# Attention in head pairs: row-tiled scores, plain fp32 attend on column tiles, normalising moved to the output

## The reference, cut to what matters

```python
q2 = (q @ wiq.T + biq).reshape(N, H, D).transpose(1, 0, 2)     # N = 384, H = 16, D = 64
k2 = (k @ wik.T + bik).reshape(N, H, D).transpose(1, 0, 2)
v2 = (v @ wiv.T + biv).reshape(N, H, D).transpose(1, 0, 2)
scores = jnp.einsum('hnd,hmd->hnm', q2, k2) * scale + mask[None]
attn = jax.nn.softmax(scores, axis=-1)
out = jnp.einsum('hnm,hmd->hnd', attn, v2)
out = out.transpose(1, 0, 2).reshape(N, OUT_F)
return out @ wo.T + bo
```

## Time and profile before

| what | value |
|---|---|
| runs | 538.48, 543.7, 538.8 us; median 538.8 us |
| profiled execution: span from first to last instruction | 537.0 us; what lies around it is not in the profile, and the median of the runs is 1.8 us above the span |
| busy PE / DVE / ACT / POOL over the span | 93% / 74% / 53% / 35% |
| mean granted clock of PE | 0.970 |
| end of half(11) to first matmul of the output projection | about 223.5 to 294.2 us |

### The profile page before, as it was taken

How to read it: one execution, slowest core, us unless ns; L and a number is a source line. 1 busy time by engine, 2 the same in 40 slices (tenths; PEclk the granted TensorE clock), 3 DMA queues, 4 the chain that set the end, 5 groups by cost and what they waited for, 6 DMA issues and landing times.

```text
span 537.0 us, 6836 instructions
## 1 busy us (share of the span) xinstructions
PE 496.9 (93%) x2583; PEld 439.1 (82%) x2583; DVE 399.3 (74%) x654; ACT 283.2 (53%) x406; POOL 189.5 (35%) x164
## 2 busy tenths in 40 slices
PE   3899999999999999999999999758999999999984
PEld 2899999999999987788888887646887877877772
DVE  5756989954444345589886875887898898898985
ACT  3443342423424225498886215436788688688630
POOL 5100443665564102288885822150020000000462
PEclk9999999999999999999999998759999999999988
DMA  8359566442334532302006362366869889888453
GB/s 303 134 213 385 120 264 239 158 158 89 147 94 150 194 105 78 131 1 79 1 1 234 125 237 99 136 241 233 320 249 422 342 340 414 344 304 361 162 191 119
DMA packets 21073, 106.33 MB, mean 198 GB/s; under 512 B 4864, under 2 KB 5248, under 8 KB 11312
## 3 DMA queue, kind: packets, MB, share of 16 engines
q1 hardware_dynamic: 15472, 91.53, 44.9%
q0 software_dynamic: 3696, 7.96, 4.5%
q10 hardware_dynamic: 1872, 6.39, 4.0%
HBM read 98.97 MB, written 6.91 MB: 197 GB/s over the span
## 4 chain that ended last, share of the span: by engine, by line
PE 56%; DVE 26%; ACT 9%; DMA 4%; issue 3%; POOL 1%; SPq 0%; ACTq 0%; DVEq 0%
PE ps L1156 51%; DVE lo L748 15%; ACT xg L665 3%; PE ps L1220 3%; ACT hi L569 3%; DMA raw<-in_wg 2%; DVE eqt L835 1%; ACT xg_hi L669 1%; DMA xg<-z_rows,slot_tok 1%; DVE x2sg L1069 1%; DMA z_rows<-xfb 1%; DVE small L753 1%; PE ps L1264 1%; ACT x2sg L674 1%; DVE ht_lo L1028 1%
## 5 line engine op out<-in xcount | busy, mean ns | idle before, releaser
L748 DVE TENSOR_TENSOR lo<-raw,hi 128x2048 fp32r<-128x2048 f32 x70 | 161.7, 2332 | 46.8 <-ACT hi L569 46.6
L569 ACT ACTIVATE hi<-raw 128x2048 fp32r<-128x2048 f32 x70 | 131.6, 1912 | 68.8 <-PE ps L1156 57.4
L454 POOL DMA_INDIRECT mask_rows<-colf,bits x48 | 61.8, 1287 | 93.7 <-DVE bits L843 44.2
L481 POOL TENSOR_SCALAR pr<-pr,small 128x384 f32<-128x384 f32 x48 | 59.1, 1249 | 53.5 <-DVE small L857 53.5
L1156 PE MATMUL ps<-xt_hi,hi 128*128 128x384 f32 x192 | 65.4, 341 | 2.2 <-DVE xt_lo L764 2.2
L1156 PE MATMUL ps<-xt_lo,hi 128*128 128x384 f32 x192 | 65.2, 339 | 0.0
L1156 PE MATMUL ps<-xt_hi,lo 128*128 128x384 f32 x192 | 65.1, 339 | 0.0
L1156 PE MATMUL ps<-hi,xg_hi 128*128 128x512 f32 x128 | 51.6, 403 | 5.7 <-DVE lo L748 3.9
L1156 PE MATMUL ps<-hi,xg_lo 128*128 128x512 f32 x128 | 50.9, 397 | 0.0
L1156 PE MATMUL ps<-lo,xg_hi 128*128 128x512 f32 x128 | 50.8, 397 | 0.0
L1156 PE MATMUL ps<-t_hi,hi 128*128 128x384 f32 x128 | 43.1, 337 | 0.6 <-DVE t_lo L794 0.6
(11 more groups left out here) (212 smaller groups left out, 1045.9 us busy)
## 6 DMA issues: line engine op xcount, KB each, us to landing
raw<-in_wf SPq DMA_DIRECT2D x42, 1024.0 KB, 7.0
raw<-in_wg SPq DMA_DIRECT2D x28, 1024.0 KB
xfb<-in_wf SPq DMA_DIRECT2D x6, 1024.0 KB, 7.4
src_i<-in_srcb ACTq DMA_DIRECT2D x4, 768.0 KB, 4.2
dst_i<-in_dstb ACTq DMA_DIRECT2D x4, 768.0 KB, 8.7
y_rows<-y SPq DMA_DIRECT2D x6, 512.0 KB, 3.0
xin<-in_x SPq DMA_DIRECT2D x3, 512.0 KB, 4.7
xres<-in_x SPq DMA_DIRECT2D x3, 512.0 KB, 4.1
```

What stands on the lines that cost most here:

```text
L454: pool.indirect_dma_start(out=mbuf[:, :], out_offset=bass.IndirectOffsetOnAxis(ap=bits[:, 1, g:g + 1], axis=0), in_=colf[:, 5, g:g + 1], i ...
L481: pool.tensor_scalar(pr[:, h % 3, i, :], pr[:, h % 3, i, :], rinv[:, h % 3, i:i + 1], None, ALU.mult).then_inc(normalised, 1)
L569: act.activation(hi[SLOT[c]][:, :], raws[RAW[c]], ACT.Copy).then_inc(hi_done, 1)
L748: dve.tensor_tensor(lo[SLOT[c]][:, :], raws[RAW[c]], f32(hi[SLOT[c]][:, :]), ALU.subtract).then_inc(lo_done, 1)
```

## The change

The unit of the loop becomes a pair of heads p, heads 2p and 2p+1, called a = 0 and 1.

- `scores(p, i)`: for one tile of 128 query rows, the matmuls of the two heads alternate. Head 0 uses contraction rows 0 to 63 of the array, head 1 rows 64 to 127, and they write two different banks. There are two pairs of score banks. The three tiles of a pair are issued at different places of the loop.
- `turn(p)`: eighteen transposes of `pr`, which is no longer divided by the sums, in six blocks over three banks. ACT copies blocks 0, 2, 4 out, and DVE blocks 1, 3, 5, whole, as fp32 `at`: there is no hi and lo of P any more.
- `attend(p)`: six plain fp32 matmuls of 384 columns with the 64 value columns of one head as weights; head 0 writes PSUM partitions 0 to 63 and head 1 partitions 64 to 127 of one bank, `SUMMED`. v is kept whole (`val`), copied by ACT and DVE.
- The reciprocals of a pair are stored by SP to memory as rows, a store of 768 elements of 4 bytes, and read back as a broadcast over 64 partitions for each head (`inv_rows`). DVE multiplies the attended pair with them (`on`), and `t_hi` and `t_lo` are written from that for all 128 rows at once. POOL's divisions are gone.
- SP's loop over the pairs stands ahead of the residual loads. Chunk 26 of the weights is split after the attention, no longer during it, and the load of chunk 29 moves behind the residual loads.

```diff
-            for c in range(GNN_CHUNKS + 2):
+            for c in range(GNN_CHUNKS + 1):
                 load(c)
...
+            for p in range(PAIRS):
+
+                sp.wait_ge(inverse_ready, p + 1)
+                sp.dma_start(ibuf[p].rearrange("a (i q) -> q a i", q=P), rinv[:, p % 2, :, :],
+                             allow_slow_non_contiguous=True).then_inc(inverse_out, 16)
+                sp.wait_ge(inverse_out, 16 * (p + 1))
+                if p >= 2:
+                    sp.wait_ge(o_scaled, p - 1)
+                for a in range(2):
+                    sp.dma_start(inv_rows[HD * a:HD * (a + 1), p % 2, :], ibuf[p, a].partition_broadcast(HD)).then_inc(inverse_in, 16)
             sp.wait_ge(score_ready, NT * HEADS)
...
+            load(GNN_CHUNKS + 1)
...
-            for h in range(HEADS):
-                for i in range(NT):
-                    if i < 2:
-                        pool.wait_ge(inverse_ready, 2 * h + i + 1)
-                    pool.tensor_scalar(pr[:, h % 3, i, :], pr[:, h % 3, i, :], rinv[:, h % 3, i:i + 1], None,
-                                       ALU.mult).then_inc(normalised, 1)
...
+            for p in range(PAIRS + 1):
+                if p < PAIRS:
+                    for m, a, j in blocks(p)[0::2]:
+                        act.wait_ge(p_turned, m + 1)
+                        act.activation(at[:, a, j, :], TURNED[j][:, 0:N], ACT.Copy).then_inc(at_act, 1)
+                if p >= 1:
+                    act.wait_ge(o_scaled, p)
+                    act.activation(t_hi[:, p - 1, :], on[:, :], ACT.Identity, bias=gbias[:, 5, p - 1:p]).then_inc(o_hi_done, 1)
+                if p + 1 < PAIRS:
+                    exps(p + 1, 2)
+                if p + 2 < PAIRS:
+                    exps(p + 2, 0)
+                    exps(p + 2, 1)
+            split_hi(OUT_LAST - 1)
             split_hi(OUT_LAST)
...
+            maxima(1, 1)
+            for p in range(PAIRS + 1):
+                if p < PAIRS:
+                    for m, a, j in blocks(p)[1::2]:
+                        dve.wait_ge(p_turned, m + 1)
+                        dve.tensor_copy(at[:, a, j, :], TURNED[j][:, 0:N]).then_inc(at_dve, 1)
+                if p >= 1:
+                    dve.wait_ge(o_ready, p)
+                    dve.wait_ge(inverse_in, 32 * p)
+                    if p >= 2:
+                        dve.wait_ge(o_lo_done, p - 1)
+                    dve.tensor_tensor(on[:, :], SUMMED[:, 0:N], inv_rows[:, (p - 1) % 2, :], ALU.mult).then_inc(o_scaled, 1)
+                if p + 1 < PAIRS:
+                    maxima(p + 1, 2)
+                if p + 2 < PAIRS:
+                    maxima(p + 2, 0)
+                if p >= 1:
+                    dve.wait_ge(o_hi_done, p)
+                    dve.scalar_tensor_tensor(out=t_lo[:, p - 1, :], in0=on[:, :], scalar=gbias[:, 5, p - 1:p], in1=f32(t_hi[:, p - 1, :]),
                                              op0=ALU.add, op1=ALU.subtract).then_inc(o_lo_done, 1)
+                if p + 1 < PAIRS:
+                    inverse(p + 1)
+                if p + 2 < PAIRS:
+                    maxima(p + 2, 1)
+            split_lo(OUT_LAST - 1)
             split_lo(OUT_LAST)
             split_lo(GNN_CHUNKS)
...
+            def scores(p, i):
+
+                n, tok = NT * p + i, slice(i * P, (i + 1) * P)
+                if n >= 2:
+                    pe.wait_ge(score_max, 2 * (n - 1))
+                for step, (s, m) in enumerate(((0, 0), (0, 1), (1, 0))):
+                    for a in range(2):
+                        rows = slice(HD * a, HD * (a + 1))
+                        ins = pe.matmul(SCORES[n % 2][a][:, 0:N], (q_hi, q_lo)[s][rows, p, tok], (k_hi, k_lo)[m][rows, p, :],
+                                        start=step == 0, stop=step == 2)
+                        if step == 2:
+                            ins.then_inc(score_ready, 1)
+
+            def turn(p):
+                pe.wait_ge(exp_done, 6 * (p + 1))
+                for m, a, j in blocks(p):
+                    if m >= 3:
+
+                        pe.wait_ge((at_act, at_dve)[(m - 3) % 2], (m - 3) // 2 + 1)
+                    for i in range(NT):
+                        ins = pe.transpose(TURNED[j][:, i * P:(i + 1) * P], pr[:, p % 2, a, i, j * P:(j + 1) * P], ident[:, :])
+                    ins.then_inc(p_turned, 1)
+
+            def attend(p):
+
+                if p >= 1:
+                    pe.wait_ge(o_scaled, p)
                 for j in range(NT):
+                    for a in range(2):
+                        m = 6 * p + 3 * a + j
+                        pe.wait_ge((at_act, at_dve)[m % 2], m // 2 + 1)
+                        cut = slice((2 * p + a) * HD, (2 * p + a + 1) * HD)
+                        ins = pe.matmul(SUMMED[HD * a:HD * (a + 1), 0:N], val[:, j, cut], at[:, a, j, :], start=j == 0, stop=j == NT - 1)
                 ins.then_inc(o_ready, 1)
...
+            scores(0, 0)
+            half(11, (0, 1))
+            pe.wait_ge(v_act, 1)
+            pe.wait_ge(v_dve, 1)
+            scores(0, 1)
+            half(11, (2, 3))
+            scores(0, 2)
+            half(11, (4, 5))
+            scores(1, 0)
+            half(11, (6, 7))
+            scores(1, 1)
+            scores(1, 2)
+            pe.wait_ge(v_act, 4)
+            pe.wait_ge(v_dve, 2)
+            for p in range(PAIRS):
+                turn(p)
+                if p + 2 < PAIRS:
+                    scores(p + 2, 0)
+                attend(p)
+                if p + 2 < PAIRS:
+                    scores(p + 2, 1)
+                    scores(p + 2, 2)
```

More of the change, by code:

```diff
@@ L45 @@
 HD = D // HEADS
+PAIRS = HEADS // 2
 EDGES = 6144
@@ L307, in gnn_ffn, with blocks @@
         TOK_BANK = [B[2], B[4]] + [B[7]] * (NE - 2)
-        SCORES, TURNED = B[3:6], [B[1], B[2], B[0]]
+        SCORES, TURNED, SUMMED = [(B[0], B[7]), (B[1], B[2])], B[4:7], B[3]
         def banks(group):
-            if group == 11:
-                return [B[6], B[7], B[0]]
+            if group >= 10:
+                return B[1:4] if group == 10 else B[4:7]
             return B[0:4] if group % 2 == 0 else B[4:8]
+        def blocks(p):
+            return [(6 * p + 3 * a + j, a, j) for a in range(2) for j in range(NT)]
         X_HALVES = [(half, t) for half in range(2) for t in range(NT)]
@@ L589, in evac @@
                 if NAMES[m] == "v2":
-                    for t in range(NT):
-                        act.activation(v_hi[:, t, h * CW:(h + 1) * CW], banks(group)[t][:, :], ACT.Copy).then_inc(bank_hi, 1)
+                    for t in (0, 2):
+                        act.activation(val[:, t, h * CW:(h + 1) * CW], banks(group)[t][:, :], ACT.Copy).then_inc(v_act, 1)
                     return
@@ L1174, in weight, with half @@
                 return hi[SLOT[c]][:, w], lo[SLOT[c]][:, w]
-            def half(i, parts=(0, 1)):
+            def half(i, steps=range(KT)):
                 m, h = HALVES[i]
@@ L1180, in half @@
                     pe.wait_ge(group_evacuated, group - 1)
-                for part in parts:
+                for part in range(2):
+                    if part * CK not in steps and (part + 1) * CK - 1 not in steps:
+                        continue
                     c = 2 * i + part
@@ L1191, in half @@
                         k = CK * part + kk
+                        if k not in steps:
+                            continue
                         if NAMES[m] == "v2":
                             for t in range(NT):
[L1194 to L1195 removed]
                                 tok = slice(t * P, (t + 1) * P)
@@ L1214, in turn @@
-            def turn(h):
-                pe.wait_ge(normalised, NT * (h + 1))
-                for j in range(NT):
-                    if h > 0:
-                        pe.wait_ge(at_lo_done, 3 * (h - 1) + j + 1)
-                    for i in range(NT):
-                        ins = pe.transpose(TURNED[j][:, i * P:(i + 1) * P], pr[:, h % 3, i, j * P:(j + 1) * P], ident[:, :])
-                    ins.then_inc(p_turned, 1)
-            def attend(h):
-                if h >= 2:
-                    pe.wait_ge(o_lo_done, h - 1)
-                pair = slice((h // 2) * P, (h // 2 + 1) * P)
-                for j in range(NT):
-                    pe.wait_ge(at_lo_done, 3 * h + j + 1)
-                    ins = three(B[6 + h % 2][:, 0:N], (v_hi[:, j, pair], v_lo[:, j, pair]),
-                                (at_hi[:, h % 2, j, :], at_lo[:, h % 2, j, :]), j == 0, j == NT - 1)
+                    if (part + 1) * CK - 1 in steps:
+                        ins.then_inc(chunk_used, 1)
@@ L1235, in _ @@
                 half(i)
-            scores(0)
-            half(11, (0,))
-            scores(1)
-            half(11, (1,))
-            scores(2)
-            pe.wait_ge(group_evacuated, 12)
-            for h in range(HEADS + 1):
-                if h < HEADS:
-                    turn(h)
-                if h >= 1:
-                    attend(h - 1)
-                if h + 3 < HEADS:
```

(4 more changed lines are left out.)

137 lines of the change are left out of this document (47 added, 90 removed).

## The result

The changed kernel takes 563.58 us, the median of four runs (563.13 to 564.28), beside 538.64 us for the kernel before in the same job: a ratio of 1.042 (95% interval 1.037 to 1.048). It is slower by 25 us, and above the range of the prediction. The profiled execution has a span of 561.4 us.

A forecast was written before the change was run, and what follows sets the result against it. PE's column passes were taken to bound the attention stage, then a loop over PE, ACT and DVE. Terms -8.4 - 0.6 + 0.1 + 3.0 = -5.9 us on 537.0 gave 531.1, with 1.8 around it 533; range 528.5 to 545.

The forecast's parts named there:

- the row trip: Reciprocals stored to memory and read back: 4 us store, 2.5 reads, 0.9 SP issues, hidden in the loop.
- a store over 7.2 us makes SP the loop: SP waits for each pair's store, so above 7.2 us its queue would set the pace.
- rival 3: In SP's queue, the store of 4-byte elements takes 8 us, SP's loop 8.9 us; kernel 543.6 us; chance 0.10.
- the stage: From the end of half(11) to the first output projection matmul: 62.3 us against 70.7, 8.4 us less.
- the loop: Per pair of heads, a closed chain of waits over PE, ACT and DVE: 8.1 us.
- attend: Six plain fp32 matmuls per pair, the two heads on two column tiles of PE: 2.4 us with the tile change.
- the second head's first slot: In attend, the heads' passes overlap except at the ends: seven slots, 2.24 us, at 0.32 us a pass.
- Before it: Ahead of the stage, four score groups of 0.8 us replace two inside the v2 projection: 0.6 us less.
- Chunk 26: Weights split only after the attention, so PE loses 0.1 to 0.8 us in the output projection; 0.1 taken.
- The expert biases: Loads behind the residual's addition, clearing and SP's issues, landing 21 us after the first projection matmul.
- the 3.0 us: PE's stall at the router, waiting for late small loads: about 3 us, 1 to 7 by the store's ends.
- the parts named for "same": Chance of a time within about 1%: rest of the forecast, rivals 1 and 4, half of rival 3; given as 0.37.

The follow-up runs named there:

- Experiment 5: Changed kernel, storing only one head's sums of one token tile (128 neighbouring 4-byte pieces), scaling rows read from x: 548.15 us.
- experiment 3: Changed kernel with each pair's reciprocals stored as 128 runs of 24 bytes instead of 768 of 4, rows in wrong order: 530.64 us.
- experiment 10: The kernel of experiment 8, with POOL clearing the bias rows before it waits for the residual and adds the bias: 526.58 us.
- experiment 1: Changed kernel without the store and reads of the rows, the attended pair multiplied with ones: 527.47 us.
- experiment 9: The kernel of experiment 8, with six residual loads (3 MB) issued between the store and reads of the seventh pair: 535.58 us.
- experiment 8: Changed kernel with sums stored as 256 pieces of 12 bytes and a multiplication reading every third element: 530.63 us; its repeat 530.77 us.

## Why the prediction was wrong

**The step that failed** is in the row trip: "I take 4 us for the store and 2.5 for the reads, with 0.9 for SP's issues; the ends are 2 and 8 for the store." The store measured 7.9 to 11.9 us, in the middle 9.7. The sentence behind it, "a store over 7.2 us makes SP the loop", is the one that came true, and rival 3 is its mechanism, at a chance of 0.10 and with a store of 8 us. Its price was too low as well: with 9.8 us for the store and 1.4 for SP's issues behind it, SP's loop is 11.2 us and not 8.9, and eight of these make 89.7 of the stage's 92.7 us.

The rows for a better size were there. A store of 128 elements of 4 bytes had let GpSimd wait 6.2 us, and I took a value nearer to the 1.9 beside it and to the plain store's 2.3, though mine had six times the pieces. Experiment 5, with 128 pieces, took 7.8 us. With 6.2 as the lower end, and the threshold of 7.2 just above it, SP's loop would have had the larger chance, and not 0.10. What no row could show is that the pieces' neighbourhood decides: the same 768 pieces, 64 bytes apart, land in 2.5 us.

The Trainium skill warns of such stores: a strided last dimension becomes one descriptor for each element (DMA: Bandwidth & Descriptors, Rules for kernel authors), and transfers under 512 bytes are read, modified and written back (the same page, Specifications). The direction is what the trace shows. But by these two rules the four stores of 768 pieces of 4 bytes should be slow alike, and the runs have 2.5 to 4.3 us for three of them and 9.7 for the fourth.

**What held, measured where the trip is fast.** In experiment 3 the stage takes 59.7 us (223.6 to 283.3) against the forecast's 62.3, and the kernel 530.6 against 533. One pair of heads in experiment 10, with a store of 12-byte pieces; PE, then ACT, then DVE in order of time:

```profile
252.67 2.16 PE L1252 MATMUL ps<-at,val 128*64 128x384 f32 x12 [0.50 <-DVE on L894]
254.76 0.44 PE L1228 MATMUL ps<-k_hi,q_hi 64*128 64x384 f32 x2
...
257.92 1.20 PE L1240 MATMUL ps<-ident,pr 128*128 128x128 f32 x9 [0.70 <-ACT at L635]
...
260.34 2.16 PE L1252 MATMUL ps<-at,val 128*64 128x384 f32 x12 [0.50 <-DVE on L894]
```

```profile
256.19 0.61 ACT L609 ACTIVATE pr<-pr,small 128x384 f32<-128x384 f32 x1 [0.52 <-DVE small L856]
...
257.40 0.85 ACT L635 ACTIVATE at<-ps 128x384 f32<-128x384 f32 x2
```

```profile
255.58 0.56 DVE L856 CUSTOM_DVE_ANT_0 pr<-ps,mask 128x384 f32<-128x384 f32 x1 [0.43 <-PE ps L1228]
...
259.63 0.65 DVE L894 TENSOR_TENSOR on<-ps,inv_rows 128x384 f32<-128x384 f32 x1
```

Read from start to start, the loop closes over PE, ACT and DVE as the prediction had it: attend 2.09 us (forecast 2.4), scores until the maximum 0.82 (0.93), the maximum 0.61 (0.55), two exponentials 1.21 (1.24), the copy 0.52 (0.59), blocks 3 to 5 and DVE's last copy 1.71 (1.76), the multiplication and its hand-over 0.71 (0.64). The sum is 7.67 against 8.11; most of the difference is attend, where I had given the second head's first slot 0.32 us that it doesn't take.

The rule of the Trainium skill that a weight load overlaps matmuls in flight only when the row group differs (TensorE: Matmul & The Clock Gate, Part 3) speaks for 3.8 us an attend. The trace has 2.16 for twelve passes whose two column tiles share all rows; here the measurement decides against it.

**Before and after the stage.** Before it, 0.6 us less was forecast; from the first score matmul ahead of half(11) to the end of that half the changed kernel takes 20.5 us against 20.7, some 0.2 less. Chunk 26 waits 0.3 us on PE in the changed kernel (0.1 forecast) and up to 1.3 in experiment 1. The expert biases land 21.1 us after the first projection matmul (21 forecast), by the path named (addition, clearing, SP's issues); that is luck in part, since that matmul was itself held back by the seventh trip as the loads were by the eighth. Of the 3.0 us, 1.8 lie at the router; the other 1.2 lie ahead of it, where the granted clock is 0.61 from 316 to 318 us and chunk 26 waits. That GpSimd's order alone gives the router's wait back, and that the clock can add to it, I hadn't seen; experiment 10 shows the first, and a case of the second.

One sum of the chances is off, without bearing on the rest: the parts named for "same" add up to 0.39 (0.09 + 0.17 + 0.08 + 0.05), not 0.37.

## What to carry to other kernels

A trip through memory that transposes a few numbers had a price set by its layout here: give each partition the longest run that it can write, and let the reading engine take the stride (0.09 us a multiplication here, for 6.6 us saved on each store). A queue that waits for a store before it may go on is a loop of its own, to be summed like an engine's; and everything behind it in the queue, here the residual's loads, ends with it. When an unknown duration has a threshold at which the bound changes, work out which side the nearest row lies on before choosing a value, and look for edits that make the threshold irrelevant.

## What the runs showed of the hardware

- Small writes to memory that lie close together are slow: 768 pieces of 4 bytes land 9.7 us after their issue when they touch, 4.3 us at 8 bytes apart, 3.1 at 16 and 2.5 at 64; 128 pieces of 24 bytes that touch, 2.1 us; 128 pieces of 4 bytes that touch, 7.8.
- Two column tiles of the PE array run plain fp32 matmuls fully side by side: twelve passes of 384 columns in 2.16 us, where twelve in line at the estimated 0.32 us would take 3.8. Two row tiles do the same for the scores, 0.17 us a step for both heads.
- Small transfers behind 3 MB of loads on the same queue landed late: two reads of 96 KB up to 10.1 us after their issue in place of 2.9, a store of 3 KB after 8 us in place of 3.1 (experiment 9).
- A wait of 2.25 us of PE was followed by eight microseconds at a granted clock of 0.50, in experiment 8's repeat; in the changed kernel, a wait of 5.5 us by four at 0.64, while two waits of 2.69 and 3.23 us were followed by attends at their full pace of 2.16.
